# A graph network kernel: row ring of 25 slots in place of 20 in two edge sweeps, loop bodies of 20 groups, six held sums in place of twelve

## The chip, the core and the metric

One core of a Trainium2 chip runs the whole program in one launch. The metric is device time in microseconds (us) of that launch, lower is better; the median of three runs of the kernel before is 2812.51 us. The engines are TensorE (PE), VectorE (DVE), ScalarE (ACT), GpSimd (POOL) and SyncE (SP); transfers run on 16 DMA engines that all queues share.

## The reference, cut to what matters

```python
# 3125 nodes, 50000 edges sorted by dst, 768 columns; heads (12x64), (12x64), (1x768)
def _gat_layer(x, W, attn_l, attn_r, bias, src, dst, num_heads, head_dim, use_elu):
    z = (x @ W).reshape(N, num_heads, head_dim)
    el, er = sum(z * attn_l, -1), sum(z * attn_r, -1)
    e = leaky_relu(el[src] + er[dst], 0.2)
    ex = exp(e - segment_max(e, dst)[dst])
    alpha = ex / segment_sum(ex, dst)[dst]
    out = segment_sum(alpha[:, :, None] * z[src], dst) + z + bias
    return elu(out) if use_elu else out
x = x + gat(gat(gat(layernorm(x))))          # three layers
# then a mixture of experts: 8 experts of 192, each token to its best two
x = x + moe(layernorm(x))
```

## The kernel before, in words

Each of the three layers (l = 0, 1, 2) has a node sweep and an edge sweep. I call the edge sweeps one, two and three. The node sweep multiplies 25 blocks of 128 nodes by the layer's weights (`W[:, l]` in on-chip memory, 6 x 792 columns per layer) and POOL stores the product rows to a table in memory, 792 or 769 columns a node.

The edge sweep goes through V = 415 visits of 128 edges, in NG = 83 groups of G = 5. For each visit POOL issues one indirect DMA (line 672) that gathers the 128 source rows of the table (about 0.4 MB) into one slot of a ring. The ring has U = 20 slots in four groups (`group_rows`): three lie in `arena`, the fourth in the room of `W[:, 0]`, the first layer's weights. Slot k % 20 is free again when PE has finished visit k - 20, which POOL waits for at line 668 on the semaphore `s_agg`.

DVE then works group by group. In `exponents` it waits for the five gathers of the next group (`s_z`) and for PE's small products of that group (`s_er`), and forms the logits (line 1475 in sweeps one and two, 1457 in sweep three). ACT takes the exponential (822), DVE multiplies each row by its weights (1492; in sweep three it weights the one-hot matrix instead, 1498). PE adds the rows up per destination node with a one-hot matrix product (`add_up`, line 1047). Five visits in 20 (six in sweep three) are done in two rounded parts instead of one full-precision product: ACT rounds (781), DVE forms the rest (1509). PE also makes, three groups ahead (`ER_LEAD`), 15 small products a group (1022) from one-hot tables that DVE makes (1445). ACT empties a node block when its last visit is done (`close_blocks`, `close`): it copies the sums out (810), clears the bank (814) and stores the sums to `mixed[l]`.

Every engine runs the 83 groups as a first part, a loop whose body holds NBUF = 4 groups (one lap of the ring) and a rest. POOL's gathers are written out one by one, without a loop.

In sweep three the sums of the last HELD = 12 blocks stay in `W` as well (`held_sums`), so the second layer norm, which follows, need not load them. That stage goes through the 25 blocks: SP loads the kept residual rows (line 556) and, for the first 13 blocks, the sums from `mixed[2]` (line 551, `load_sums`); DVE adds the two (1589) and takes moments; ACT stores the result to `out` and normalises; POOL stores the normalised rows. Each sums load for a block b of 5 or more waits until the store of block b - 5 has landed, since they share a buffer. Then come the routing on DVE and the experts on PE.

Of the kernel before, what the change touches and what calls it, by code (L numbers as in the profile page):

```python
# [16 lines left out]
N, D = 3125, 768  # L17
# [12 lines left out]
U = G * NBUF  # L30
# [3 lines left out]
NI = -(-NG // NBUF)  # L34
LAST_GROUPS = NG - (NI - 1) * NBUF
# [11 lines left out]
HELD = 12  # L47
# [52 lines left out]
def gnn_ffn(nc, x, edges, gnn, ffn, out):  # L100
    with ExitStack() as ctx:
# [67 lines left out]
        b_g = sb("b_g", [1, NG, 4], I32)  # L169
        b_of = sb("b_of", [1, NG + ER_LEAD, 8], I32)  # L170
        ends = sb("ends", [1, NB], I32)
        turns = sb("turns", [1, NS], I32)
# [136 lines left out]
        def group_rows(l, jj):  # L309

            w = slot_width(l)
            if jj < IN_ARENA:
                home = arena[:, jj * G * w:(jj + 1) * G * w]
            else:
                home = W[:, 0, :, :].rearrange("p k n -> p (k n)")[:, 0:G * w]
            return home.rearrange("p (u n) -> p u n", u=G)

        def edge_row(l, at):
            return group_rows(l, at // G)[:, at % G, :]

        def edge_heads(l, jj, n=1):
            return group_rows(l, jj)[:, :, D:D + n * HEADS[l]]
# [13 lines left out]
        def split_before(l):  # L336
            left_out = [sum(at >= LAST_GROUPS * G for at in x) for x in SPLIT[:l]]
            return NI * sum(len(x) for x in SPLIT[:l]) - sum(left_out)

        def uses(jj):  # L340

            return NI if jj < LAST_GROUPS else NI - 1
# [28 lines left out]
        def held_sums(b):  # L371

            return flat_W[:, bass.ds((b % HELD) * D + W_REST, D)]
# [208 lines left out]
        def _(pool):  # L582
# [70 lines left out]
            for l in range(3):  # L653
# [13 lines left out]
                for k in range(V):  # L667
                    pool.wait_ge(s_agg, V * l + k + 1)
                    if l == 2 and k == 12 * D // slot_width(l):
# [3 lines left out]
                        edge_row(l, k % U)[:, 0:table_width(l)], None, table[l][:, :],  # L673
                        bass.IndirectOffsetOnAxis(src_k[:, k:k + 1].bitcast(U32), 0)).then_inc(s_z[k % U], 16)

# [15 lines left out]
        def _(act):  # L691
# [72 lines left out]
            def edge_sweep(l):  # L764
                H = HEADS[l]

                def leading(g, i, jj):

                    for j in range(G):
# [4 lines left out]
                        row = edge_row(l, at)  # L774
# [4 lines left out]
                        act.wait_ge(s_agg, U * i + (V * l + at + 1))  # L779
# [38 lines left out]
                def weights(g, jj):  # L818
# [3 lines left out]
                    nc.scalar.activation(edge_heads(l, jj), wt[:, jj, :, 0:H], ACT.Exp).then_inc(s_exp, 1)  # L822
# [14 lines left out]
                def body(i, last, first=False):  # L837
                    groups = LAST_GROUPS if last else NBUF
                    for jj in range(groups):
                        g = NBUF * i + jj  # L840
                        leading(g, i, jj)
                        if not (last and jj == groups - 1):
                            weights(g + 1, (jj + 1) % NBUF)
                        if jj or not first:
                            close_blocks(g - 1)
                        if H > 1 and (not last or jj + 2 < groups):
                            one_hots(g + 2, (jj + 2) % NBUF)
# [7 lines left out]
                with act.Fori(1, NI - 1) as i:  # L855
                    body(i, False)
                body(NI - 1, True)
# [71 lines left out]
        def _(pe):  # L929
# [74 lines left out]
            def edge_sweep(l):  # L1004
# [23 lines left out]
                def add_up(g, i, jj, j, b):  # L1028

                    at = jj * G + j  # L1030
                    odd = (b + l) % 2
                    flat = PS[:, :, :].rearrange("p b n -> p (b n)")
                    if at in SPLIT[l]:
                        n = SPLIT[l].index(at)
                        pe.wait_ge(s_rest, len(SPLIT[l]) * i + (n + 1 + split_before(l)))
                        onehot = S[:, jj, j, :]
                        rows = [parts[:, n, part, :] for part in range(2)]
                    else:
                        pe.wait_ge(s_msg, g * G + (V * l + j + 1))
                        onehot = f32(S[:, jj, j, :]) if H > 1 else S_weighted[:, jj, j, :]  # L1040
                        rows = [edge_row(l, at)]
# [9 lines left out]
                def body(i, last):  # L1051
                    groups = LAST_GROUPS if last else NBUF
                    for jj in range(groups):
                        g = NBUF * i + jj
                        ahead = not last or jj + ER_LEAD < groups
                        now = blocks_of(g)
                        for j in range(G):
                            add_up(g, i, jj, j, now[j])
# [11 lines left out]
                with pe.Fori(0, NI - 1) as i:  # L1070
                    body(i, False)
                body(NI - 1, True)
# [787 lines left out]
```

## Time and profile before

| | us |
|---|---|
| median of three runs | 2812.51 (2811.25 to 2815.1) |
| span of the profiled execution | 3059.8 |
| node sweep one and preparation (0 to 262) | 262 |
| edge sweep one (262 to 902) | 640 |
| node sweep two (902 to 1115) | 213 |
| edge sweep two (1115 to 1763) | 648 |
| node sweep three (1763 to 1963) | 200 |
| edge sweep three (1963 to 2610) | 647 |
| second layer norm and routing (2610 to 2730) | 120 |
| experts (2730 to 3060) | 330 |

The profiled execution has a span of 3059.8 us, 247 us more than the median of the runs without a profile; its own time outside the profiler is not given. The difference has to be kept in mind: stage times of the trace are those of that one, slower execution. A row of busy time names line, engine, operation, tiles, count, busy time, mean time of one, and the idle time ahead of it with what ended it.

### The profile page before, as it was taken

The numbers are of one execution on the slowest core, as the hardware profiler recorded it, in microseconds if no ns is written. First come the engines' busy times: TensorE is split into PE (matmuls) and PEld (weight loads), VectorE is DVE, ScalarE is ACT, GpSimd is POOL, SyncE is SP. The second block draws the span as 40 slices with busy tenths as digits, with TensorE's granted clock in tenths as the row PEclk, the third lists the DMA queues.
The fourth block names the chain that finished last, engine by engine and source line by source line (L and its number), as shares of the span: only waits on it lengthen the run. The fifth ranks groups of instructions, "written<-read, shape, count | busy, mean of one in ns | idle before, by whom it ended". The sixth has DMA issues, their size and how long they took to land.

```text
span 3059.8 us, 57119 instructions
## 1 busy us (share of the span) xinstructions
PE 2691.3 (88%) x14056; PEld 1838.6 (60%) x14060; DVE 2096.8 (69%) x3895; ACT 1244.9 (41%) x2607; POOL 1506.0 (49%) x1528
## 2 busy tenths in 40 slices
PE   3997999998989979898989999788898889759998
PEld 2884555555558855555555578555555555547776
DVE  6776888888887768888878877545555555673332
ACT  1224555555544435555555544223222223622211
POOL 1005666666631156666666412466666665114443
PEclk9998999999999979999999999899999999979999
DMA  6447888888867878888888767788888887967776
GB/s 210 169 148 251 289 286 291 291 290 290 289 219 205 210 228 292 289 287 290 291 287 288 250 191 216 218 281 285 279 282 281 282 282 258 397 217 145 145 146 118
DMA packets 199261, 762.09 MB, mean 249 GB/s; under 512 B 41889, under 2 KB 58033, under 8 KB 198542
## 3 DMA queue, kind: packets, MB, share of 16 engines
q0 software_dynamic: 127632, 604.14, 64.8%
q1 hardware_dynamic: 53790, 108.21, 11.6%
q10 hardware_dynamic: 17760, 48.79, 4.0%
q8 instruction: 36, 0.59, 0.1%
q14 instruction: 43, 0.35, 0.0%
HBM read 640.01 MB, written 133.45 MB: 253 GB/s over the span
## 4 chain that ended last, share of the span: by engine, by line
PE 50%; DVE 21%; issue 13%; ACT 4%; DMA 4%; another core or an unknown queue 3%; SPq 2%; POOL 1%; DVEq 1%; ACTq 1%; POOLq 0%
PE PS L1047 30%; DVE arena L1492 5%; PE PS L1176 5%; PE PS L978 4%; PE PS L1165 4%; PE PS L980 2%; DVE parts L1509 2%; PE PS L1022 2%; DMA arena<-table,src_k 2%; SPq L493 1%; DVE ST_b L1445 1%; DVE arena L1357 1%; DVE arena L1367 1%; DVE arena L1335 1%
## 5 line engine op out<-in xcount | busy, mean ns | idle before, releaser
L672 POOL DMA_INDIRECT arena<-table,src_k x945 | 959.9, 1016 | 500.8 <-issue 213.1
L1047 PE MATMUL PS<-arena,S 128*128 128x384 f32 (+1 forms) x1848 | 706.8, 514 | 57.8 <-issue 46.3
L1492 DVE TENSOR_TENSOR arena<-arena,PS 128x768 f32<-128x768 f32 x630 | 575.2, 946 | 0.9 <-ACT arena L822 0.9
L1047 PEld LDWEIGHTS PS<-arena,S 128*128 128x128 f32 x1848 | 335.5, 194 | 282.7 <-issue 156.8
L1047 PE MATMUL PS<-parts,S 128*128 128x384 f32 (+2 forms) x1332 | 340.4, 375 | 57.2 <-issue 51.0
L672 POOL DMA_INDIRECT W<-table,src_k x300 | 295.9, 986 | 160.5 <-PE PS L1047 71.2
L1047 PE MATMUL PS<-arena,S_weighted 128*128 128x384 f32 (+1 forms) x840 | 319.9, 516 | 33.4 <-issue 25.3
L1022 PEld LDWEIGHTS PS<-erp,ST_b 128*128 128x128 bf16 x3735 | 193.9, 97 | 249.9 <-issue 184.2
L618 POOL DMA_DIRECT2D table<-arena x75 | 41.6, 555 | 557.7 <-DVEq L1379 382.3
L1047 PEld LDWEIGHTS PS<-parts,S 128*128 128x128 f32 x1332 | 223.7, 192 | 106.0 <-issue 97.5
L830 ACT ACTIVATE apart<-iota_row,dst_k 128x128 f32<-128x128 f32 x830 | 261.7, 389 | 60.8 <-issue 44.1
L781 ACT ACTIVATE parts<-arena 128x780 fp32r<-128x780 f32 x168 | 142.0, 849 | 309.2 <-DVE arena L1492 136.7
L1022 PE MATMUL PS<-erp,ST_b 128*128 x3735 | 213.0, 172 | 54.0 <-issue 38.9
L1047 PE MATMUL PS<-W,S 128*128 128x396 f32 (+1 forms) x640 | 239.8, 502 | 14.6 <-issue 8.1
L1047 PEld LDWEIGHTS PS<-arena,S_weighted 128*128 128x128 f32 x840 | 154.3, 196 | 143.7 <-issue 79.4
L978 PE MATMUL PS<-W_lead,S 128*128 128x512 f32 x450 | 190.4, 423 | 9.8 <-DVE xT_rest L1383 7.9
L1509 DVE TENSOR_TENSOR parts<-arena,parts 128x780 fp32r<-128x780 f32 x168 | 162.0, 964 | 35.7 <-issue 24.4
L1492 DVE TENSOR_TENSOR W<-W,PS 128x768 f32<-128x768 f32 x200 | 182.4, 944 | 0.0
L978 PE MATMUL PS<-W_lead,xT_rest 128*128 128x512 f32 x450 | 179.2, 398 | 0.0
L978 PE MATMUL PS<-W_rest_r,S 128*128 128x512 f32 x450 | 178.7, 397 | 0.0
L1047 PEld LDWEIGHTS PS<-W,S 128*128 128x128 f32 x640 | 116.1, 190 | 91.3 <-issue 39.0
L1795 DVE TENSOR_SCALAR arena<-PS,gate_of 128x768 f32<-128x768 f32 x56 | 57.0, 1018 | 162.5 <-PE PS L1176 162.5
(293 smaller groups left out, 4354.1 us busy)
## 6 DMA issues: line engine op xcount, KB each, us to landing
arena<-mixed SPq DMA_DIRECT2D x63, 384.0 KB, 3.6
table<-arena POOLq DMA_DIRECT2D x50, 396.0 KB, 3.3
local_b<-local SPq DMA_DIRECT2D x123, 160.0 KB
mixed<-sums ACTq DMA_DIRECT2D x50, 384.0 KB
arena<-table SPq DMA_DIRECT2D x50, 384.0 KB, 4.6
arena<-table,src_k POOLq DMA_INDIRECT x945
table<-arena POOLq DMA_DIRECT2D x25, 384.5 KB, 4.6
out<-last_bias POOLq DMA_DIRECT2D x25, 384.0 KB, 6.4
```

Source lines behind the costliest of these rows:

```text
L672: nc.gpsimd.indirect_dma_start(edge_row(l, k % U)[:, 0:table_width(l)], None, table[l][:, :], bass.IndirectOffsetOnAxis(src_k[:, k:k + 1]. ...
L781: nc.scalar.activation(parts[:, n, 0, 0:D + H], row[:, 0:D + H], ACT.Copy).then_inc(s_leading, 1)
L830: o = nc.scalar.activation(apart[:, j, :], iota_row[:, :], ACT.Abs, scale=-1.0, bias=dst_k[:, bass.ds(g * G + j, 1)])
L978: nc.tensor.matmul(PS[:, 4 + 2 * b.q, :], rows[x_part], W_parts[W_part][:, 0:512], start=start, stop=stop)
L980: o = nc.tensor.matmul(PS[:, 5 + 2 * b.q, 0:z_width(l) - 512], rows[x_part], W_parts[W_part][:, 512:z_width(l)], start=start, stop=stop)
L1022: o = nc.tensor.matmul(er_of(l, jj)[:, j, :], ST_b[:, jj, j * P:(j + 1) * P], erp[:, bass.ds(b * (6 * H) + part * 2 * H, 2 * H)], start=(p ...
L1047: o = nc.tensor.matmul(flat[:, bass.ds(odd * 1024 + 512 * c, n)], onehot, row[:, c * HALF:c * HALF + n], start=False, stop=True, skip_grou ...
L1165: o = nc.tensor.matmul(to, token_xT(b.q)[:, k * P:(k + 1) * P], WiT[:, k, bass.ds(e * FF, FF)], start=(k == 0), stop=(k == KC - 1))
L1176: o = nc.tensor.matmul(PS[:, 4 + 2 * b.q + c, 0:HALF], hT(b.q)[0:rows, j * P:(j + 1) * P], flat[0:rows, bass.ds(e * (2 * D) + (2 * c + j) ...
L1492: nc.vector.tensor_tensor(z, z, a, ALU.mult).then_inc(s_msg, 1)
L1509: nc.vector.tensor_tensor(low[:, 0:D + H], row[:, 0:D + H], f32(high[:, 0:D + H]), ALU.subtract).then_inc(s_rest, 1)
L1795: nc.vector.tensor_scalar(zr(b.q, D).rearrange("p (c d) -> p c d", c=2), PS[:, 4 + 2 * b.q:6 + 2 * b.q, 0:HALF], gate_of[:, bass.ds(b.n, 1 ...
```

## The change

In edge sweeps two and three the ring has 25 slots, five groups (`ROW_GROUPS = (4, 5, 5)`). The fifth group lies in `W`: in sweep two in the room of the second layer's weights `W[:, 1]`, in sweep three from column `W_REST` on. To make that room the held sums shrink from 12 blocks to 6, at the end of `W`. Sweep one keeps 20 slots. Since all other buffers still turn over four groups, the smallest stretch that repeats is lcm(4, 5) = 20 groups, so the loop bodies in sweeps two and three are 20 groups long (`PERIOD`). Some index tables become bytes in place of 32-bit words, for room.

```diff
+ROW_GROUPS = (4, 5, 5)
+U = G * max(ROW_GROUPS)
+PERIOD = tuple(math.lcm(NBUF, n) for n in ROW_GROUPS)
+BODIES = tuple(-(-NG // n) for n in PERIOD)
+IN_LAST = tuple(NG - (n - 1) * p for n, p in zip(BODIES, PERIOD))
-HELD = 12
+HELD = 6
-        b_of = sb("b_of", [1, NG + ER_LEAD, 8], I32)
+        b_of = sb("b_of", [1, NG + ER_LEAD, 8], U8)
...
+            elif jr == IN_ARENA:
+                home = flat_W[:, 0:G * w]
             else:
-                home = W[:, 0, :, :].rearrange("p k n -> p (k n)")[:, 0:G * w]
+                at = KC * (D + 2 * HMAX) if l == 1 else W_REST
+                home = flat_W[:, at:at + G * w]
...
-            return flat_W[:, bass.ds((b % HELD) * D + W_REST, D)]
+            return flat_W[:, bass.ds((b % HELD) * D + (3 * KC * (D + 2 * HMAX) - HELD * D), D)]
...
-                    pool.wait_ge(s_agg, V * l + k + 1)
+                    pool.wait_ge(s_agg, V * l + k + 1 + AHEAD - slots(l))
...
-                with act.Fori(1, NI - 1) as i:
+                with act.Fori(1, BODIES[l] - 1) as i:
...
-                with pe.Fori(0, NI - 1) as i:
+                with pe.Fori(0, BODIES[l] - 1) as i:
...
-                with dve.Fori(1, NI - 2) as i:
-                    dc.enter(i - 1, (1 if H > 1 else 3) * NBUF)
+                with dve.Fori(1, BODIES[l] - 2) as i:
+                    dc.enter(i - 1, (1 if H > 1 else 3) * PERIOD[l])
```

`AHEAD` is U and is added to `s_agg` once at the start, so it goes from 20 to 25; POOL's wait in sweep one and every other wait on `s_agg` mean the same visit as before, and in sweeps two and three POOL waits for visit k - 25. `HELD`, `NBUF`, the buffers of the one-hot matrices and `ER_LEAD` do not turn with the row ring.

In sweeps two and three PE's loop goes from 20 turns to 4, ACT's from 19 to 3 and DVE's from 18 to 2. In the built program PE's loop body of sweep two grows from 275 instructions to 1,355 and DVE's from 66 to 318 (sweep three: from 114 to 558).

POOL's program at the start of sweep two. `arena` and `W` are the homes of the slots, `table` and `src_k` the rows and their numbers. Before:

```order
L672 DMA arena<-table,src_k 128x792 [waits s_tables,s_filled,s_tab,s_stored0,s_stored1,s_agg]
L672 DMA arena<-table,src_k 128x792 [waits s_agg] x14
L672 DMA W<-table,src_k 128x792 [waits s_agg] x5
L672 DMA arena<-table,src_k 128x792 [waits s_agg] x15
L672 DMA W<-table,src_k 128x792 [waits s_agg] x5
```

After:

```order
L696 DMA arena<-table,src_k 128x792 [waits s_tables,s_filled,s_tab,s_stored0,s_stored1,s_agg]
L696 DMA arena<-table,src_k 128x792 [waits s_agg] x14
L696 DMA W<-table,src_k 128x792 [waits s_agg] x10
L696 DMA arena<-table,src_k 128x792 [waits s_agg] x15
L696 DMA W<-table,src_k 128x792 [waits s_agg] x10
```

Each lap now has ten gathers into `W` in place of five; the number of gathers and their order are the same.

SP's program in the second layer norm, from the load for the last block whose sums are not held. Before (`out` holds the kept rows, `mixed` the sums):

```order
L551 DMA arena<-mixed 128x768 [waits s_turnable,s_kept_x21,s_sums_st]
L556 DMA arena<-out 128x768 [waits s_summed]
L551 DMA arena<-mixed 128x768 [waits s_turnable,s_kept_x22,s_sums_st]
L556 DMA arena<-out 128x768 [waits s_summed] x12
L572 DMA W<-in_L_ffn_Wi 128x9216 [waits s_kept_x22,s_kept_x23,s_kept_x21,s_kept_x24,s_kept_x20,s_turnable]
```

After:

```order
L575 DMA arena<-mixed 128x768 [waits s_turnable,s_kept_x22,s_sums_st]
L580 DMA arena<-out 128x768 [waits s_summed]
L575 DMA arena<-mixed 128x768 [waits s_turnable,s_kept_x23,s_sums_st]
L580 DMA arena<-out 128x768 [waits s_summed] x6
L596 DMA W<-in_L_ffn_Wi 128x9216 [waits s_kept_x22,s_kept_x23,s_kept_x21,s_kept_x24,s_kept_x20,s_turnable]
```

Six loads of sums are new, each with its wait for the buffer, and each of them stands between two loads of kept rows.

## Rows read from the trace of the kernel before

**Rows 1.** Busy time by stretch: stretch, length, each engine's busy us, clock, DMA share.
```profile
core 0: us, PE busy (x) PEld busy (x) DVE busy (x) ACT busy (x) POOL busy (x), PEclk, DMA share, GB/s
1115.00:1763.00 648.00, 574.56 (x2860) 345.11 (x2860) 539.74 (x775) 351.23 (x833) 410.22 (x408) 0.98 0.86 283
1963.00:2610.00 647.00, 570.42 (x2860) 348.98 (x2860) 346.24 (x1085) 186.06 (x408) 406.16 (x409) 0.97 0.86 279
2612.00:2672.00 60.00, 44.79 (x317) 31.91 (x318) 45.31 (x122) 39.25 (x72) 9.83 (x18) 0.90 1.03 414
```

**Rows 2.** Chain of waits, 1225 to 1256 us: start, us, what.
```profile
1234.67 0.95 POOL arena L672
...
1238.66 7.95 DMA arena<-table,src_k
```

**Rows 3.** Timeline of POOL in sweep two: start, us, operation, idle before and its releaser.
```profile
1403.14 0.94 POOL L672 DMA_INDIRECT W<-table,src_k  x1 [0.30 <-issue]
1404.39 1.00 POOL L672 DMA_INDIRECT W<-table,src_k  x1 [0.30 <-PE PS L1047]
1405.69 0.95 POOL L672 DMA_INDIRECT W<-table,src_k  x1 [0.30 <-issue]
1408.29 0.95 POOL L672 DMA_INDIRECT W<-table,src_k  x1 [1.65 <-remote]
1409.55 0.94 POOL L672 DMA_INDIRECT arena<-table,src_k  x1 [0.30 <-issue]
```

**Rows 4.** Timeline of DVE in the same stretch.
```profile
1408.00 0.34 DVE L1475 SCALAR_TENSOR_TENSOR wu<-arena,shift,PS 128x120 f32<-128x120 f32 x1 [1.04 <-remote]
...
1415.89 0.34 DVE L1475 SCALAR_TENSOR_TENSOR wu<-W,shift,PS 128x120 f32<-128x120 f32 x1 [1.75 <-remote]
```

**Rows 5.** What ended DVE's idle time before line 1475, sweep two: us, times.
```profile
  remote: 71.7, 40
  DMA arena<-table,src_k: 13.6, 9
  DMA W<-table,src_k: 1.2, 1
```

**Rows 6.** The same for line 1457 in sweep three.
```profile
  remote: 150.5, 57
...
  DMA arena<-table,src_k: 10.6, 4
  DMA W<-table,src_k: 2.1, 1
```

**Rows 7.** Who PE waited for, sweep two, then sweep three: total us, times, longest.
```profile
PE PS L1047 <- DVE arena L1492: 10.0, 10, 3.2
...
PE PS L1047 <- DVE parts L1509: 3.4, 3, 2.1
```
```profile
PE PS L1047 <- DVE S_weighted L1498: 6.9, 6, 5.7
...
PE PS L1047 <- DVE parts L1513: 1.0, 1, 1.0
```

**Rows 8.** Timeline of DVE in the second layer norm, line 1589.
```profile
2618.04 0.97 DVE L1589 SCALAR_TENSOR_TENSOR arena<-arena,den 128x768 f32<-128x768 f32 x1
...
2649.47 1.02 DVE L1589 SCALAR_TENSOR_TENSOR arena<-arena,den 128x768 f32<-128x768 f32 x1 [1.88 <-DMA arena<-mixed]
2651.85 0.97 DVE L1589 SCALAR_TENSOR_TENSOR W<-W,den,arena 128x768 f32<-128x768 f32 x1
2654.19 0.98 DVE L1589 SCALAR_TENSOR_TENSOR W<-W,den,arena 128x768 f32<-128x768 f32 x1
...
2687.64 1.02 DVE L1589 SCALAR_TENSOR_TENSOR W<-W,den,arena 128x768 f32<-128x768 f32 x1
```

**Rows 9.** DMA queues of instructions over the whole span: packets, MB, share of 16 engines.
```profile
q8 instruction: 36, 0.59, 0.1%
q14 instruction: 43, 0.35, 0.0%
```

More of the change, by code:

```diff
@@ L307, in slot_width, with group_rows, row_group, edge_row @@
             return D + 2 * HEADS[l]
[L309 removed]
+        def group_rows(l, jr):
             w = slot_width(l)
[L312 to L315 removed]
+            if jr < IN_ARENA:
+                home = arena[:, jr * G * w:(jr + 1) * G * w]
+            elif jr == IN_ARENA:
+                home = flat_W[:, 0:G * w]
+            else:
+                at = KC * (D + 2 * HMAX) if l == 1 else W_REST
+                home = flat_W[:, at:at + G * w]
             return home.rearrange("p (u n) -> p u n", u=G)
[L318 to L322, printed above, removed]
+        def row_group(l, r):
+            return r % ROW_GROUPS[l]
+        def edge_row(l, r, j):
+            return group_rows(l, row_group(l, r))[:, j, :]
+        def edge_heads(l, r, n=1):
+            return group_rows(l, row_group(l, r))[:, :, D:D + n * HEADS[l]]
+        def slots(l):
+            return G * ROW_GROUPS[l]
+        def landed(l, i, r, j):
+            slot = row_group(l, r) * G + j
+            before = sum(len(range(slot, V, slots(m))) for m in range(l) if slot < slots(m))
+            return s_z[slot], 16 * (PERIOD[l] // ROW_GROUPS[l]) * i + 16 * (before + r // ROW_GROUPS[l] + 1)
+        def lap_of(l, i, r):
+            return (PERIOD[l] // NBUF) * i + r // NBUF
         def group_bank(jj):
@@ L837, in body @@
                 def body(i, last, first=False):
[L838 to L844, printed above, removed]
+                    groups = IN_LAST[l] if last else PERIOD[l]
+                    for r in range(groups):
+                        g = PERIOD[l] * i + r
+                        leading(i, r)
+                        if not (last and r == groups - 1):
+                            weights(i, r + 1)
+                        if r or not first:
                             close_blocks(g - 1)
-                        if H > 1 and (not last or jj + 2 < groups):
-                            one_hots(g + 2, (jj + 2) % NBUF)
+                        if H > 1 and (not last or r + 2 < groups):
+                            one_hots(g + 2, (r + 2) % NBUF)
                 if H > 1:
@@ L1051, in body @@
                 def body(i, last):
[L1052 to L1055, printed above, removed]
+                    groups = IN_LAST[l] if last else PERIOD[l]
+                    for r in range(groups):
+                        g, jj = PERIOD[l] * i + r, r % NBUF
+                        ahead = not last or r + ER_LEAD < groups
                         now = blocks_of(g)
                         for j in range(G):
-                            add_up(g, i, jj, j, now[j])
+                            add_up(i, r, j, now[j])
                             if j == 0 and ahead:
@@ L1454, in logits @@
                         dve.wait_ge(s_er, g + (NG * l + 1))
-                        for j in range(jj * G, (jj + 1) * G):
-                            dve.wait_ge(s_z[j], 16 * i + 16 * (uses(jj) * l + 1))
-                        dc.mark(nc.vector.tensor_tensor(u, edge_heads(l, jj), er[:, :, 0:H], ALU.add))
+                        for j in range(G):
+                            dve.wait_ge(*landed(l, i, r, j))
+                        dc.mark(nc.vector.tensor_tensor(u, edge_heads(l, r), er[:, :, 0:H], ALU.add))
                     def leaky():
@@ L1554, in edge_sweep @@
                     dc.link(o)
-                for step in exponents(0, 0, 0):
+                for step in exponents(0, 0):
                     step()
```

101 lines of the change are left out of this document (53 added, 48 removed).

## The prediction, made before the changed kernel ran

> **What bounds the kernel now.** I first split the span by stage, then asked in the two changed sweeps who waits for the gathers, and last looked at the layer norm, which pays for the room.
>
> Sweeps two and three last 648 and 647 us for 415 visits each, 1.56 us a visit [rows 1]. PE is busy 575 and 570 us of that, so even a ring without limit can't give back more than 73 and 77 us. DVE is busy 540 us in sweep two but only 346 in sweep three, and the two last equally long; so DVE's amount of work does not set the pace alone. The DMA engines are at 0.86, which is 557 us of work: a second floor just under PE's. The reader should see three resources close together, none quite full.
>
> Does the ring bind? POOL can issue a gather every 1.25 us when nothing holds it (0.95 busy and 0.30 between) and needs one every 1.56. It does stop: at 1405.69 it issues and then stands 1.65 us, until 1408.29 [rows 3]. That is the wait for PE to free a slot, so the ring is full at times. But a full ring costs only if the rows then come too late. DVE's logits stand at 1408.00 and 1415.89 [rows 4]. The second one is for the slots in `W`, whose last gather was issued at 1408.29: 7.6 us earlier. The longest landing that I find on the chain took 7.95 us [rows 2] and it is an exception; so ordinarily the rows have landed before they are asked for. The waits of the logits named as ended by a gather are 13.6 + 1.2 = 14.8 us in sweep two [rows 5] and 12.7 us in sweep three [rows 6]. Far more, 71.7 and 150.5 us, is ended by something the profile has no name for. The logits wait for two things, five gathers and PE's small products. I take the unnamed part as mostly PE's: POOL, which waits for PE alone, stops and goes on within 0.3 us of the same moments, 1408.00 and 1408.29, and one of its own pauses is unnamed too. That is an inference, and the first rival is that it's wrong.
>
> **The terms.** The profiled execution is 247 us longer than the median, so I take differences from the trace and add them to 2812.5; the terms are small enough that scaling them by 0.92 changes nothing.
>
> Ring, sweeps two and three. A gather may start five visits, 5 x 1.56 = 7.8 us, earlier. That covers nearly every named late landing. Bounds: no gain at all, if PE's stock of finished rows hides each wait of DVE; at most the named waits, 27.5 us. PE's idle time put down to DVE is 13.4 us in sweep two and 7.9 in sweep three [rows 7], 21.3 together, and a part of it has other causes (ACT's rounding, closing of blocks). I take 8 us, nearer the low end, since PE's rows are the ones that set the end. After that the next late thing is PE's own work.
>
> Held sums. In the layer norm the DMA engines are at 1.03 and 414 GB/s from 2612 to 2672 [rows 1]. Blocks whose sums are loaded go by at (2649.47 - 2618.04) / 8 = 3.93 us; held ones at (2687.64 - 2649.47) / 12 = 3.18 us, and at 2.34 us when nothing is late [rows 8]. Six blocks change kind. Low end 6 x 0.75 = 4.5 us, high end 6 x 1.59 = 9.5 us. A third way: six transfers of 0.393 MB at 414 GB/s are 5.7 us of full DMA time. I take +6. The new loads stand in SP's queue ahead of loads of kept rows, and these wait with them; that is how it goes for the first 13 blocks already, so the 3.93 contains it. Nothing covers this: the expert weights are loaded behind it and routing follows the last block.
>
> Loop edges. PE goes from 20 turns to 4, DVE and ACT likewise, so 16 edges fewer a sweep. The trace shows no stop at an edge that I can name; nearest is the 0.30 us between two gathers of POOL, and 2 x 16 x 0.30 = 9.6 us would be the most. It runs beside engine work in PE's queue. I take -1; zero is the other end.
>
> Code. The longer bodies have to be fetched: some 6,000 built instructions more over PE, ACT and DVE. Before, instruction packets are 79 with 0.94 MB in all [rows 9], a thousandth of the traffic; twice as much is still nothing in bandwidth. A stop at the few edges that remain is another matter (below). I take +3 for it, between 0 and the price of the second rival, 12 to 24.
>
> Byte tables, one more column of ones to clear, one more semaphore group: the same number of instructions per group, and I take nothing; a few tenths of a us either way.
>
> Sum: -8 + 6 - 1 + 3 = 0. Forecast: **2812 us, no change that can be measured**.
>
> A rule against the change. Rows 9 shows 36 and 43 instruction packets in the whole span while the three sweeps' PE loops take 57 edges. The Trainium skill (Runtime: NRT & Kernel Launch, Instruction fetch mechanics) says that an engine holds 512 instructions, TensorE 2,048, and that a taken branch to a page that is not held stops the engine for a DMA fetch. By that rule the small bodies stayed, and the trace agrees: the packets are too few for a fetch each turn. The new bodies of ACT and of DVE in sweep three would not stay, by the same rule, and PE's is at the limit. What it would cost is the second rival.
>
> **Rivals.**
> *The gathers are what the unnamed waits wait for.* For it: POOL does stop on a full ring, and a ring loop stands on the chain, POOL's issue followed by 7.95 us of landing [rows 2]. Against it: the 7.6 us between last gather and logits. If half of the 71.7 + 150.5 + 27.5 = 250 us of DVE's waits shrank and PE gained a quarter of that, the ring would give 31 us: 2812.5 - 31 + 8 = about 2790. It decides when a gather's landing takes over 7 us more often than the chain shows.
>
> *Code fetched at every turn.* Per sweep PE has 3 taken edges, ACT 2, DVE 1: 12 in all. Instruction packets of queue 8 take 0.1% of 16 x 3059.8 us, 49 us over 36 packets, 1.4 us each with the rounding's 0.7 to 2. If a stop of 1 to 2 us at each reaches PE, that is 12 to 24 us; with +6 for the sums, -1 and a gain of 4 by the ring: 2825 to 2838, say **2830**. It decides if a body is larger than what the engine holds, and it is slower than before.
>
> *The ring gives nothing.* Where it stops, PE is the slower one, and PE sees none of the late gathers. Then the sum is +6 and up to +3: about 2820, slower by 0.27%. For it: PE waits for DVE in only 10 and 6 cases [rows 7]. Against it: the chain does run through a gather.
>
> *That it does not do what it says* is hardly open: POOL's pace of 1.25 against 1.56 us fills five slots more within some 25 visits.
>
> **How the numbers follow.** Forecast (terms cancel) 0.36, 2807 to 2818. Gathers decide 0.31, about 2790. Ring gives nothing 0.18, about 2820. Code stops 0.15, about 2830. The range must leave out at most 0.2: from 2790 to 2834; below lies about a third of the first rival with a larger gain, above a part of the last. A measurement of this kernel tells about 0.2%, 5.6 us, from no change. Faster by more: 0.31. Within: 0.36. Slower by more: 0.33.
>
> **What would show it.** Step by step in the profile after: sweep one (unchanged but for the byte tables) within 3 us of 640. Waits of the logits named as ended by a gather nearly gone in sweeps two and three, the unnamed ones as large as before, and the sweeps shorter by 3 to 5 us each. POOL's pauses in number like before, since the pace is PE's. In the layer norm blocks 13 to 18 at 3.9 us, the stage 6 us longer. Instruction packets about twice as many; many more than that, with stops of PE every 20 groups, would be the second rival. I'm wrong if the unnamed waits fall with the named ones (first rival), or if PE's idle time doesn't move and only the layer norm does (third).

## The result, and the profile after

The changed kernel takes 3063.76 us (median of 4 runs, 3056.45 to 3070.23), the kernel before 2811.88 us (4 runs, 2806.32 to 2815.1). The ratio is 1.089, 95% interval 1.0867 to 1.0914: **9% slower, by 252 us**. The forecast was 2812, the range ended at 2834.

The profiled execution of after has a span of 3054.8 us, like its runs. The one of before had 3059.8 against runs of 2812. So the two traces are equally long, and put side by side they do not show the loss. That alone says that the trace I read before predicting was not of the condition in which the time was measured; what differed is found further down.

First, by stage. This is the table of busy time by stretch for after, the three edge sweeps and the first 60 us of the layer norm (columns as in [rows 1]):

```profile
core 0: us, PE busy (x) PEld busy (x) DVE busy (x) ACT busy (x) POOL busy (x), PEclk, DMA share, GB/s
264.00:893.00 629.00, 571.36 (x2860) 332.06 (x2859) 533.90 (x770) 347.63 (x828) 405.94 (x405) 0.99 0.87 289
1104.00:1754.00 650.00, 578.56 (x2866) 336.24 (x2865) 538.36 (x775) 347.90 (x832) 408.19 (x407) 0.97 0.85 283
1955.00:2596.00 641.00, 565.30 (x2861) 334.49 (x2861) 340.81 (x1086) 184.44 (x407) 403.70 (x408) 0.98 0.85 281
2600.00:2660.00 60.00, 39.26 (x289) 28.31 (x289) 40.23 (x107) 35.59 (x65) 9.25 (x17) 0.95 1.03 413
```

Sweep one has neither the larger ring nor the longer bodies and still lasts 629 us. Outside of the three sweeps the kernel takes 2834 - 1697 = 1137 us in the trace of the control below, so a time of 2812 leaves (2812 - 1137) / 3 = 558 us for each sweep. Whatever costs 9% acts in all three sweeps. Of the parts of the change only the tables do that. Here is TensorE's load of block numbers into registers, the line in `blocks_of`, first in the trace of before, then in that of after (count: shortest/median/longest in ns):

```profile
L1012 PEldq TENSOR_LOAD <-b_of x498: 5/582/1751, 249.9 to 2596.9; - x166
```
```profile
L1038 PEldq TENSOR_LOAD <-b_of x498: 1216/1222/2645, 251.6 to 2584.3; - x166
```

The same 498 loads of five numbers each, twice a group. From 32-bit words one takes 582 ns, from bytes 1222 ns: 498 x 0.64 = 319 us more in the one sequence of instructions that feeds the matrix engine.

The queues of instructions, which stood at 36 and 43 packets [rows 9]:

```profile
q8 instruction: 113, 1.85, 0.2%
q14 instruction: 111, 0.91, 0.1%
```

Nearly three times as many, not twice: the 20-group bodies are fetched while the loop runs. The stop can be seen at the end of TensorE's loop. This is the branch there in sweep two, for the control below (a lap of 4 groups, 20 turns) and for after (20 groups; shortest/median/longest in ns):

```profile
L1070 PEldq COMPARE_BRANCH  x20: 76/208/211, 1079.8 to 1596.2; - x20
```
```profile
L1097 PEldq COMPARE_BRANCH  x4: 79/4067/4582, 1261.6 to 1734.0; - x4
```

Three of the four last 3.9, 4.2 and 4.6 us, and in sweep three three more last 4.7 to 6.1 us; all six together are 29 us. Here is the first of them in PE's timeline (start, us, operation, idle before and what ended it):

```profile
1261.58 1.56 PE L1074 MATMUL PS<-W,S 128*128 128x384 f32 x4
1268.69 4.46 PE L1074 MATMUL PS<-arena,S 128*128 128x384 f32 x8 [5.56 <-ACT S L860]
```

PE has reached group 20. The branch starts at 1261.58 and takes 3.92 us, a load of block numbers behind it 2.45 us, and PE goes on at 1268.69. The profile puts the wait down to ACT's one-hots (line 860), which were ready at 1268.09. But ACT had itself stood 4.99 us until PE's last sum before the branch:

```profile
1263.50 0.18 ACT L830 ACTIVATE den<-PS  x1 [4.99 <-PE PS L1074]
```

What ended the idle time before the logits, which were lines 1475 and 1457 in [rows 5, 6] and are 1503 and 1485 now, sweep two and then sweep three:

```profile
  PE PS L1048: 67.2, 51
  DMA arena<-table,src_k: 6.0, 4
```
```profile
  PE PS L1048: 111.5, 46
  DMA arena<-table,src_k: 26.9, 9
  DMA W<-table,src_k: 8.1, 3
```

Where before had 71.7 and 150.5 us of unnamed waits, after has 67.2 and 111.5 us that PE's small products of line 1048 ended. The named gather waits went from 14.8 to 6.0 us in sweep two and from 12.7 up to 35.0 in sweep three.

And the layer norm (line 1589 in [rows 8] is 1617 now), blocks 4, 13, 18, 19 and 24:

```profile
2605.45 0.96 DVE L1617 SCALAR_TENSOR_TENSOR arena<-arena,den 128x768 f32<-128x768 f32 x1
...
2640.85 1.02 DVE L1617 SCALAR_TENSOR_TENSOR arena<-arena,den 128x768 f32<-128x768 f32 x1 [1.03 <-DMA arena<-mixed]
...
2660.45 1.02 DVE L1617 SCALAR_TENSOR_TENSOR arena<-arena,den 128x768 f32<-128x768 f32 x1 [1.59 <-DMA arena<-mixed]
2662.84 0.97 DVE L1617 SCALAR_TENSOR_TENSOR W<-W,den,arena 128x768 f32<-128x768 f32 x1
...
2680.85 1.02 DVE L1617 SCALAR_TENSOR_TENSOR W<-W,den,arena 128x768 f32<-128x768 f32 x1
```

(2660.45 - 2640.85) / 5 = 3.92 us a block for 13 to 18, as priced. From block 4 to block 24 it is 75.4 us, where [rows 8] gives 2687.64 - 2618.04 = 69.6: 5.8 us more.

### The profile page after: what moved, and what is told of

It is laid out like the page before. It is cut to its first block, busy times and chain, and to the rows that moved or that the text cites. A ratio compares the mean times of both kernels' runs of the same rounds, so it can differ in the third digit from the quotient of the medians.

```text
span 3054.8 us, 56139 instructions
## 1 busy us (share of the span) xinstructions
PE 2676.8 (88%) x14056; PEld 1798.4 (59%) x14060; DVE 2087.2 (68%) x3896; ACT 1240.2 (41%) x2607; POOL 1499.6 (49%) x1528
## 4 chain that ended last, share of the span: by engine, by line
PE 52%; DVE 21%; issue 9%; DMA 7%; ACT 5%; POOL 2%; SPq 2%; ACTq 1%; DVEq 1%; POOLq 0%
PE PS L1074 32%; PE PS L1203 5%; DVE arena L1521 4%; PE PS L1004 4%; PE PS L1192 4%; PE PS L1006 2%; DVE W L1521 2%; DMA arena<-table,src_k 2%; PE PS L1048 2%; POOL arena L696 2%; DMA W<-table,src_k 2%; DVE parts L1538 2%; SPq L517 1%; DVE arena L1384 1%; DVE arena L1362 1%
## 5 line engine op out<-in xcount | busy, mean ns | idle before, releaser
L696 POOL DMA_INDIRECT arena<-table,src_k x825 | 830.7, 1007 | 428.3 <-PE PS L1074 279.4
L1074 PE MATMUL PS<-arena,S 128*128 128x396 f32 (+1 forms) x1688 | 659.1, 517 | 89.1 <-DVE arena L1521 32.0
L1521 DVE TENSOR_TENSOR arena<-arena,PS 128x768 f32<-128x768 f32 x570 | 520.1, 945 | 0.9 <-ACT arena L848 0.9
L696 POOL DMA_INDIRECT W<-table,src_k x420 | 417.5, 994 | 202.1 <-PE PS L1074 135.3
L1074 PEld LDWEIGHTS PS<-arena,S 128*128 128x128 f32 x1688 | 303.7, 193 | 310.1 <-issue 194.8
L1074 PE MATMUL PS<-W,S 128*128 128x384 f32 (+1 forms) x800 | 309.6, 511 | 29.6 <-issue 12.9
L1074 PE MATMUL PS<-arena,S_weighted 128*128 128x384 f32 x712 | 273.0, 515 | 43.6 <-issue 21.0
L1521 DVE TENSOR_TENSOR W<-W,PS 128x768 f32<-128x768 f32 x260 | 237.2, 944 | 0.0
L1048 PE MATMUL PS<-erp,ST_b 128*128 x3735 | 183.2, 171 | 23.8 <-DVE ST_b L1472 16.4
L1074 PE MATMUL PS<-W,S_weighted 128*128 128x384 f32 x448 | 168.3, 503 | 14.5 <-issue 8.4
```

What stands on the lines that cost most here:

```text
L696: nc.gpsimd.indirect_dma_start(edge_row(l, k // G, k % G)[:, 0:table_width(l)], None, table[l][:, :], bass.IndirectOffsetOnAxis(src_k[:, k ...
L1048: o = nc.tensor.matmul(er_of(l, jj)[:, j, :], ST_b[:, jj, j * P:(j + 1) * P], erp[:, bass.ds(b * (6 * H) + part * 2 * H, 2 * H)], start=(p ...
L1074: o = nc.tensor.matmul(flat[:, bass.ds(odd * 1024 + 512 * c, n)], onehot, row[:, c * HALF:c * HALF + n], start=False, stop=True, skip_grou ...
L1521: nc.vector.tensor_tensor(z, z, a, ALU.mult).then_inc(s_msg, 1)
```

## The experiments

**Theories.** *Byte tables*: the longer register loads hold up TensorE's sequence in all sweeps. *Code*: bodies of 20 groups are fetched at every turn. *Ring*: gathers issued earlier disturb something. *Held sums*: +6.

One thing has to be said of the machines, or the numbers can't be read. The experiments ran on five chips, and these are of two kinds for this kernel. On three of them before takes 2804 to 2810 us, on two others 3035 and 3062. The difference is seen in TensorE's register operations. Those of line 1022 (1048 after) in the trace of before that I predicted from, then in the kernel before with masks (below), once on a chip of either kind:

```profile
L1022 PEldq FUSED_REGOPS  x3735: 2/46/728, 250.8 to 2588.8; - x197
```
```profile
L1022 PEldq FUSED_REGOPS  x3735: 46/46/52, 250.6 to 2358.6; - x197
```
```profile
L1022 PEldq FUSED_REGOPS  x3735: 2/46/1384, 251.6 to 2611.3; - x197
```

The medians agree. On the second kind single ones last some 0.7 us: counted over all of TensorE's register operations, 216 over 0.4 us in the trace of before (146 us together) and 225 in the third trace; none in the second, and none in any other trace from the first kind of chip. I call the kinds *even* and *stalling*. Two executions of one kernel, the second packed one below, show that the time goes there: with 264 such operations and with none, the times from the start of one register operation of TensorE to the start of the next add up to 1924 and 1684 us. That is 239 us of the 269 by which the stalling execution is longer, though the long operations themselves are only 176. The result, 1.089, was measured on an even chip: before took 2812 us there, and the trace of after has none. Each run below is compared with before on its own chip.

### Which part costs 9%: four kernels on an even chip

**The byte tables alone.**
```diff
-        b_g = sb("b_g", [1, NG, 4], I32)
-        b_of = sb("b_of", [1, NG + ER_LEAD, 8], I32)
+        b_g = sb("b_g", [1, NG, 4], U8)
+        b_of = sb("b_of", [1, NG + ER_LEAD, 8], U8)
-        turns = sb("turns", [1, NS], I32)
+        turns = sb("turns", [1, NS], U8)
```


> The kernel before with the three tables (b_of, b_g, turns) as bytes and nothing else: ring of 20, bodies of 4 groups, 12 held sums. Byte theory: TensorE's load of five block numbers into registers took a median of 582 ns in the trace of before and 1222 ns in the trace of after, twice a group, 249 loads of each kind over three sweeps; 498 x 0.64 = 319 us of its sequencer, of which some is covered, so this kernel takes 3030 to 3090 us. Code theory (the loop bodies of 20 groups are fetched again at every turn; ring and tables cost nothing): 2812, within 5. The byte theory is wrong if the time is under 2850.

Measured: 3019.81 against 2803.73, ratio 1.0769 (1.075 to 1.0787), +216 us. A little under the range given, far over 2850.

**A control for kernels with word tables**, whose loaded numbers are kept within bounds by a mask.
```diff
-                    pool.wait_ge(s_added[(n + 1) % 2], changed + 16 * ((n - 1) // 2))
+                    pool.wait_ge(s_added[(n + 1) % 2], (changed & 16) + 16 * ((n - 1) // 2))
-                        with act.Fori(lo, hi) as b:
+                        with act.Fori(lo & 31, hi & 31) as b:
-                    pe.wait_ge(s_acc_free, b + (NB * l + 1))
+                    pe.wait_ge(s_acc_free, (b & 31) + (NB * l + 1))
```


> A control for the kernels that keep 32-bit tables here: the kernel before, in which the loaded block numbers are passed through 'and 31' (for 'turns' 'and 16') before a wait or a loop bound uses them. The values are the same; on TensorE it adds up to five register operations a group. Both theories: 2812 to 2835, from nothing to 166 x 5 operations of some 25 ns. What it measures over 2812 is taken off the other kernels with this mask.

Measured: 2831.77, ratio 1.0091 (1.0074 to 1.0109), +28 us. TensorE has 1245 register operations more.

**The changed kernel with word tables** (the same masks, the three tables `I32` again).


> The changed kernel with the three tables as 32-bit words again (masked as in the control); ring of 25, bodies of 20 groups and six held sums stay. Byte theory: the loss is gone, 2800 to 2840, and TensorE's register loads last 0.58 us again. Code theory: still 3000 or more.

Measured: 2874.38, ratio 1.0253 (1.0233 to 1.0272): 71 over before, 43 over the control. That is 34 us above the range that the byte theory gave: the tables are most of the loss, not all of it.

**Only `b_of` as bytes** (`b_g` and `turns` masked words).


> The kernel before with b_of alone (the table that TensorE loads twice a group) as bytes, b_g and turns as masked words. Byte theory, narrower form: the whole loss is TensorE's, so this is as slow as the kernel with all three tables as bytes, 3030 to 3090. Byte theory, wider form (each engine loses a part): about halfway, 2900 to 3000. Code theory: as the control.

Measured: 3019.35, ratio 1.0767 (1.0749 to 1.0785), the same as with all three. So what the tables cost is in TensorE's loads alone. The table of stretches for sweep two, control and then byte tables:

```profile
1046.00:1615.00 569.00, 547.91 (x2860) 328.26 (x2860) 537.25 (x772) 347.86 (x830) 407.49 (x407) 0.99 0.91 321
```
```profile
1104.00:1740.00 636.00, 572.82 (x2866) 332.89 (x2866) 536.92 (x772) 348.33 (x830) 410.79 (x407) 0.98 0.86 288
```

In the control PE is busy 548 and DVE 537 of 569 us; with bytes DVE does the same 537 in 636 and the DMA share falls from 0.91 to 0.86. What PE waited for there, again control and then bytes (us, times, longest):

```profile
PE PS L1047 <- issue: 7.1, 23, 0.7
```
```profile
PE PS L1047 <- issue: 27.6, 55, 2.0
```

"Issue" is idle time that no other engine ended. It grows by 20 us; another 25 us appear as longer busy time of PE, whose ends are modelled, and 17 as waits for DVE. DVE does the same work, but its logits wait 28 us for PE's small products with bytes, and in the control not at all.

The loss does not begin at once. By the starts of DVE's logits the byte kernel keeps level with the control through the first 12 groups of sweep two and from group 16 to 80 falls behind by 58 us, 0.9 us a group, of the 1.28 us by which its two loads are longer.

### On a stalling chip

**Bodies of 20 groups alone** (the changed kernel's code with ring 20, twelve held sums, masked words).
```diff
-ROW_GROUPS = (4, 5, 5)
+ROW_GROUPS = (4, 4, 4)
-PERIOD = tuple(math.lcm(NBUF, n) for n in ROW_GROUPS)
+PERIOD = (4, 20, 20)
-HELD = 6
+HELD = 12
```


> The ring stays at 20 slots and twelve sums are held, tables are masked words as in the control; only the loop bodies of sweeps two and three are unrolled to 20 groups. With words, the changed kernel was 43 us above the control. Theory A (the bodies cost it, by code that is fetched at every turn): 2865 to 2875, so 33 to 38 above the control, all in sweeps two and three. Rival (the ring costs it: gathers issued earlier disturb something else): as the control, 2832.

**Six held sums alone.**
```diff
-HELD = 12
+HELD = 6
-            return flat_W[:, bass.ds((b % HELD) * D + W_REST, D)]
+            return flat_W[:, bass.ds((b % HELD) * D + (3 * KC * (D + 2 * HMAX) - HELD * D), D)]
```


> Six held sums instead of twelve and nothing else, with masked word tables as in the control. The prediction priced this at 6 (six blocks of the last LayerNorm stage at 3.93 in place of 3.18 us gives 4.5, and 1.5 for its start): 2836 to 2840. Rival (its loads are covered): 2832.

Measured: 3069.17 and 3060.21 against 3035.4, ratios 1.0113 (1.0097 to 1.0129) and 1.0077 (1.0062 to 1.0091). The expected times were for an even chip and say nothing here. The control was run on the other stalling chip only: 1.0056. Against that the bodies cost 0.6% and the held sums 0.2%, which is 6 us, between chips and so only roughly.

**`b_of` as 16-bit numbers**, on the same chip.


> The kernel before with b_of as 16-bit numbers, b_g and turns as masked words. If the price is one of elements narrower than a word, TensorE's load of five lasts 1.22 us again and the time is 3020; if it is one of bytes alone, 0.58 us and 2805 to 2830; between them if it goes by the width.

```profile
L1013 PEldq TENSOR_LOAD <-b_of x498: 13/1222/2795, 249.6 to 2606.5; - x166
```

Measured: 3071.03, ratio 1.012 (1.0104 to 1.0136). The load's median is 1222 ns as with bytes: its price is that of elements narrower than a word. But the kernel loses 1.2%, not 7.7. Its trace has 46 register operations over 0.4 us, where the held-sums kernel on the same chip has 221. On a stalling chip the long loads cost less, and most of the stalls are gone with them; how the one brings about the other is not shown.

**One load a group, packed.** Meant to beat both kernels.
```diff
-                    return nc.values_load_multi_w_load_instructions(
-                        b_of[0:1, bass.ds(g, 1), 0:G].rearrange("o i j -> o (i j)"), engines=[mybir.EngineType.PE],
+                def load_words(g, slot):
+                    nc.reg_load(words[slot], b_of[0:1, bass.ds(g, 1), 0:2].rearrange("o i j -> o (i j)"))
+                def block(slot, j):
+                    word = words[slot][j // 3]
+                    ...
+                        nc.tensor.reg_alu(shifted, word, 5 * (j % 3), ALU.logical_shift_right)
+                        nc.tensor.reg_alu(out, shifted, 31, ALU.bitwise_and)
```


> A version meant to be faster than both: from the kernel before, the five block numbers of a group are packed into two 32-bit words (five bits each), loaded once a group instead of twice five, kept in registers of TensorE for three groups, and taken apart by shifts and masks (16 register operations a group); b_g and turns as bytes, which cost nothing in the run above. If the edge sweeps go at the pace of TensorE's own sequence of instructions: one load of two (some 0.35) in place of two of five (1.16), less 16 operations at 0.0226 (0.36, from the control), is 0.45 us a group, 249 groups: 112 at most, and 0.68 of it (as with the bytes) 76: 2690 to 2730. Rival (TensorE's matmuls or the gathers set the pace, and only a longer sequence hurts): 2795 to 2815.

Measured: 3104.94, ratio 1.0225 (1.0209 to 1.0242): slower. Its load of two words takes

```profile
L1016 PEldq TENSOR_LOAD <-b_of x249: 2/537/1672, 251.4 to 2627.1; - x125
```

537 ns, not the 350 I had assumed: a load is nearly all fixed price (two words 537, five words 582), so fewer words in one spare next to nothing.

### The same on the other stalling chip

> The changed kernel itself. In the runs so far the kernel before took 2804 to 2812 us on some chips, where no register operation of TensorE lasted over 40 ns, and 3035 on another, where 221 of them lasted some 0.7 us (as in the profile of before, 216). In the traces with byte tables there are none. If this chip is of the first kind: 3063 against 2808. If it is of the second kind: with byte tables these stalls have room in the longer loads or don't come, and this takes 3060 to 3095 against 3035, so 1 to 2% more and not 9%.

The changed kernel: 3125.85 against 3061.97, ratio **1.0213** (1.0194 to 1.0232). The same change costs 9% on an even chip and 2% on this one, at the upper end of the 1 to 2% expected: its trace has 84 stalls, the control's 225, some 100 us less in long operations. (The expected text is wrong on the even chips: there register operations of TensorE last up to 0.12 us, not 0.04.)

> The control (the kernel before, loaded numbers masked), so that this batch has its own: on a chip without the stalls 2832; on one with them 3050 to 3060.

The control: 3080.79, ratio 1.0056 (1.004 to 1.0073); 19 us over before, and some 20 us above the time written, since before itself is slower on this chip.

> Bodies of 20 groups alone, ring 20, twelve held sums, masked words. On a chip without the stalls: code theory 2865 to 2872, all in sweeps two and three (sweep one as in the control, each of the others 15 to 21 us longer); ring theory 2832. With the stalls: 3065 to 3070, as in the run before, which is 10 to 15 above its control.

Bodies alone: 3091.67, ratio 1.01 (1.0083 to 1.0117), 11 us over its control.

The packed load with two operations a group fewer (shifted numbers at the top of a word go without the mask where no wait uses them):


> One load of two packed words a group in place of two loads of five, with 14 register operations a group to take them apart. The version with 16 took 3105 against 3035 on the chip with the stalls, so there its register operations cost more than its loads saved. On a chip without the stalls, by 0.0226 us an operation: 1.16 - 0.54 (its load's median in that trace) - 14 x 0.0226 = 0.31 us a group, 249 groups: 50 to 77 less than before, 2730 to 2760. Rival (operations cost their start-to-start of 0.09 us, not 0.0226): 14 x 0.09 = 1.26 a group against 0.62 saved, 160 us more: 2960.

Measured: 3105.24, ratio 1.0128 (1.0101 to 1.0154): slower here too. The times expected were for an even chip.

### Length of the sequence, bodies and packing on an even chip

**A third load of words.** Nothing is narrower, TensorE only has 249 more loads:
```diff
                         for j in range(G):
+                            if j == 3:
+                                now = blocks_of(g)
                             add_up(g, i, jj, j, now[j])
```


> Masked words, and the five block numbers of a group are loaded three times instead of twice (again ahead of its fourth visit): 249 more loads of 0.58 us, 145 us of TensorE's sequence, no byte anywhere. If what the byte table costs is the length of the sequence on TensorE, then by the 216 us for 319 us of longer loads this costs 98 us over the control on a chip without stalls (2930), and up to 145; on one with stalls 19 to 29 (3100), by the 2% there. If it is something of the bytes themselves, nothing: 2832 or 3081.

```profile
L1012 PEldq TENSOR_LOAD <-b_of x747: 578/583/1977, 250.1 to 2528.7; - x187
```
```profile
1093.00:1720.00 627.00, 582.89 (x2864) 330.24 (x2864) 540.32 (x775) 348.51 (x830) 412.16 (x407) 0.99 0.88 292
```

Measured: 2993.21 against 2809.3, ratio 1.0655 (1.0632 to 1.0678). Over the control that is 5.6% or 158 us for 249 x 0.583 = 145 us of loads; more than expected. A load takes more of the sequence than its own duration: from the start of each load to the start of the next instruction it is 516 us in all here and 335 in the control, 181 more. Of these 158 are paid, about 0.9; with bytes it is 683 us against 332, 351 more, and 216 are paid, about 0.6. Sweep two grows from 569 to 627 us like with bytes. So it is not something about bytes: loads added to TensorE's sequence are for the most part paid.

> The same kernel as e12. On a chip without stalls 2730 to 2760 if its 14 register operations a group cost what the masks did; 2960 if they cost their whole start to start. On a chip with stalls 1.3% over before again.

Packed, even chip: 2837.02, ratio 1.0097 (1.0074 to 1.0121). Both values missed: 28 over before, not 50 to 77 under it, and not 2960 either. Its sweep two lasts 572 us, the control's 569. Against before, 498 x 0.582 - 249 x 0.537 = 156 us of loads are spared and some 2,900 register operations added (13,094 for 10,226), and together they cost 28 us.

> Bodies of 20 groups alone, as in e11. On a chip without stalls 2865 to 2872 if the bodies are what the changed kernel with words had over the control (43, less 5 for the held sums), sweep one unchanged; 2832 if it is the ring. On a chip with stalls 8 to 14 over the control.

Bodies of 20 alone: 2868.14, ratio 1.0207 (1.0186 to 1.0229), within the range of the code theory. Less the control's 1.0091 that is 1.2%, 33 us. Its edge sweeps, sweep one, two, three:

```profile
263.00:830.00 567.00, 545.48 (x2860) 330.49 (x2860) 529.53 (x769) 347.85 (x828) 423.51 (x404) 0.99 0.92 321
1044.00:1631.00 587.00, 553.74 (x2860) 334.90 (x2860) 538.71 (x771) 348.30 (x830) 409.29 (x407) 0.97 0.90 313
1833.00:2409.00 576.00, 539.50 (x2860) 339.25 (x2860) 341.35 (x1084) 184.93 (x405) 414.36 (x408) 0.97 0.90 313
```

Against 569, 569 and 559 in the control: sweep one the same, the other two 18 and 17 us longer. It has 117 packets on queue 8, like after (113), and its PE has the same six long branches, 4.5 to 5.3 us each, 29.9 us together. In sweep two:

```profile
L1097 PEldq COMPARE_BRANCH  x4: 79/4810/5348, 1185.3 to 1612.1; - x4
```

By the starts of the block-number loads of sweep two PE is level with the control up to group 18, 8 us behind at group 22, 14 at 42 and 19 at 62, and loses nothing in between. So the price of the bodies is the stop at TensorE's turns.

The changed kernel with words had 1.0253. Its sweeps two and three take 591 and 575 us, so the ring takes nothing off the 587 and 576 here. It did do its work for DVE: this is what ended the idle time before the logits of sweep three, first with the ring of 20 (bodies alone), then with 25 (changed kernel with words):

```profile
  DMA arena<-table,src_k: 89.2, 43
  DMA W<-table,src_k: 14.2, 12
  PE PS L1048: 5.1, 2
```
```profile
  PE PS L1048: 50.1, 31
  DMA arena<-table,src_k: 32.6, 12
  DMA W<-table,src_k: 11.5, 5
```

103 us of gather waits became 44, DVE waited 45 us longer for PE in their place, and the sweep was no shorter. The two kernels ran on different even chips, and their profiled executions are equally long (2868.0 and 2867.9 us), so the traces do not show where the remaining 0.46% lie.

> The byte tables alone, as in e1. On a chip without stalls 7.7% over before again. On a chip with stalls: the changed kernel was 64 over before there, of which some 11 are the bodies and 5 the held sums, so 45 to 50 over before, and fewer stalls in the trace (84 in the changed kernel, 225 in the control).

Byte tables alone: 3021.71, ratio 1.0756 (1.0733 to 1.0779), as before on another even chip.

### Does a spared load give its time back

Loop bodies of 8, and of 12, groups in all sweeps; numbers loaded for three groups on are kept and used again inside a body (348 and 312 loads in place of 498). `b_g` and `turns` are bytes, `b_of` masked words.
```diff
-PERIOD = (4, 20, 20)
+PERIOD = (8, 8, 8)
+                    loaded = {}
-                        now = blocks_of(g)
+                        now = loaded[r] if r in loaded else blocks_of(g)
-                                later = blocks_of(g + ER_LEAD)
+                                later = loaded[r + ER_LEAD] = blocks_of(g + ER_LEAD)
```


> Bodies of 8 groups in all three sweeps (ring 20, twelve held sums, b_of as masked words), in which the five block numbers that TensorE loads for three groups on are kept in their registers and used again, so that 5 of 8 groups load once and not twice: about 150 loads fewer. By the third load (161 us for 249, 0.65 each) that gives back 97 from the control's 2832: 2735 to 2745 without a price of the bodies, up to 2790 with one like that of 20 groups (18 a sweep) on a chip without stalls. Rival (TensorE's sequence binds only when longer than now): 2832 or more. On a chip with stalls: 17 to 97 less than its control, so 2% either side of before.

> The same with bodies of 12 groups: 9 of 12 groups load once, about 184 loads fewer, 120 us by the same rate: 2712 to 2720 without a price of the bodies, up to 2770 with it, on a chip without stalls. If the price begins between 8 and 12 groups, this is slower than the 8-group version in place of 22 us faster.

Measured on an even chip: 2835.03 and 2816.32 against 2810.19, ratios 1.0083 (1.0058 to 1.0107) and 1.0018 (1.0003 to 1.0033). Both far above what was expected, and no kernel here beats the one before. The rival holds for the first: 150 loads spared give nothing against the control. Sweep two of the 8-group kernel, and what its PE waited for:

```profile
1046.00:1617.00 571.00, 542.74 (x2860) 341.38 (x2860) 537.15 (x772) 349.18 (x830) 411.23 (x407) 0.98 0.91 321
```
```profile
PE PS L1074 <- DVE parts L1539: 19.6, 12, 3.9
...
PE PS L1074 <- issue: 1.4, 4, 0.4
```

"Issue" fell from 7.1 to 1.4 us, so the sequence did get shorter; but waits for DVE's parts rose from 4.8 to 19.6 us, and the sweep is as long as the control's. No branch of PE lasts over 0.24 us in either kernel, so the bodies of 8 and 12 groups do not pay the stop. With 12 groups sweep two is 558 us and sweep three 560; what makes it 19 us faster than with 8 was not taken apart (its instruction packets are 57 and 142, against 42 and 94).

## Why the prediction was wrong, point by point

- **Byte tables: this step failed.** I wrote "the same number of instructions per group, and I take nothing". The number was the same, the duration was not: 582 to 1222 ns a load, 498 of them. They cost 212 to 216 us on even chips, and a third load of words, 158 us, shows that it is the time in TensorE's sequence that is paid for. I never asked what one register load takes, though the trace of before had the row. It also had a row that [rows 7] leave out, the largest of PE's idle time in sweep two:

```profile
PE PS L1047 <- issue: 45.8, 82, 5.0
```

"Issue" again: for most of its idle time PE waited for no other engine, and for DVE 13.4 us. (The control on an even chip has 7.1 us of it.) Why about 0.6 of the longer loads and 0.9 of the added ones is paid is open; that the first groups of a sweep lose nothing is a part of it.
- **The base.** "Scaling them by 0.92 changes nothing" passed over the better question, what had made that execution 247 us longer than the runs. It was on a chip whose TensorE stalls in register operations; the long ones make 146 of the 247 us, and the rest is open for this trace. The slack that I read between PE, DVE and the DMA engines [rows 1] was partly these stalls. Without them PE is busy at 548 of 569 us and DVE at 537.
- **Unnamed waits are PE's: likely, but after does not prove it.** After names line 1048, 67.2 and 111.5 us, but it ran on an even chip, and whether a wait has a name goes with the chip: the changed kernel on a stalling chip again has 66.6 us unnamed and 27.9 for line 1048 in sweep two. What speaks for PE is that there the ring of 25 left the unnamed waits as they were (the control on that chip has 70.2) while the gather waits went from 14.3 to 3.0 us. So they are hardly gathers, and since the ring gave nothing, the first rival (2790) falls. On an even chip with word tables the unnamed waits aren't there at all; the control's logits in sweep two waited only for gathers

```profile
  DMA arena<-table,src_k: 10.9, 9
  DMA W<-table,src_k: 7.6, 8
```

and in sweep three 106 us for them, though PE was busy 535 of 559 us.
- **Ring, -8: it gave nothing.** With word tables sweeps two and three are as long with the ring of 25 as with that of 20 (1166 against 1163 us), although DVE's gather waits in sweep three fell from 103 to 44 us. That PE's rows set the end was right; that 8 us of it would reach PE was not. The third rival was right on this term.
- **Code, +3: mis-sized.** The second rival had it: a stop at each turn, 12 to 24 us. Measured 33 (35 by the two sweeps), and one stop is 4 to 6 us, not 1 to 2. In after PE's six turns cost 29 us; ACT stands 4.0 to 4.5 us behind each of its four, and DVE 5.95 us at its one turn in sweep three and not at all in sweep two. PE's pace shows only its own. The Trainium skill (Runtime: NRT & Kernel Launch, Instruction fetch mechanics) says that a jump to a page that isn't held stops the engine for a fetch; 117 and 116 packets in the kernel with bodies alone, against 36 and 44 in the control, agree with it. So does DVE, whose body of 318 instructions did not stop and whose 558 did, on either side of the 512 cited in the prediction; PE's body of 1,355 stopped although it is below the 2,048 cited there, and the measurement decides.
- **Loop edges, -1: no trace of a gain.** Fewer edges, each dearer.
- **Held sums, +6: right.** 3.92 us a block, and 5.8 us more from block 4 to 24; the kernel with held sums alone came out some 6 us over the control, roughly.
- **Expected signs.** Sweep one "within 3 us of 640": it was 629, and this compared a stalled sweep with an unstalled one that has some 60 us more than the control's 569 from longer loads. Two opposite things of nearly the same size hid the loss.

Sum on an even chip, in place of 0: tables +214, bodies +33, held sums +6, ring 0, together 253 against 252 measured. That it fits to 1 us is luck: the parts come from different chips and carry some 5 us each.

## What to carry to other kernels

When a change alters the type or place of anything that an engine loads into registers, read that load's duration in the trace before calling it free, and ask whether the engine's own sequence sets the pace. When the profiled execution is longer than the runs by more than its terms, find out why before taking slack from it. Taking work off the sequence that binds gave back almost nothing here, since the waits moved to another engine, while 0.6 to 0.9 of what was added to it was paid. And when a wait at a loop's turn is put down to another engine, look at the waiting engine's own branch first.

## What the runs showed of the hardware

- A register load by TensorE of five 32-bit words takes 582 ns, of two words 537 ns; of five 8-bit or 16-bit numbers 1222 ns. On ACT a load of two bytes took 474 ns and of two words 495, so there narrow elements cost nothing.
- The branch at the end of TensorE's loop takes 0.21 us with bodies of 4 groups, at most 0.24 with 8 and 12, and 3.9 to 6.1 us with 20 (1,355 instructions in sweep two).
- On two of five chips TensorE's (and in part ACT's) register operations, 32 to 46 ns by median, now and then last 0.7 us: 177 to 264 times in a kernel whose TensorE loads words, 84 in the changed kernel and 46 with the 16-bit table. The kernel before is 8 to 9% slower there (3035 and 3062 against 2804 to 2810). What makes them, and why slower loads make them rarer, stays open.
- So the ratio of two kernels can depend on the chip: 1.089 and 1.0213 for the same pair.
